# Eight expert tiles started beside the last routing tail, two softmax inverses on VectorE, and store landings awaited one tile later

## The reference

```python
# 1. attention over pixels with 128 inner channels, then 1x1 convolutions, a residual and relu
attn = softmax(einsum('bcn,bcm->bnm', v, q), axis=2); av = einsum('bcn,bnm->bcm', k, attn)
x = relu(bn2(conv(bn1(conv(av)))) + x)
t = to_tokens(x)                                   # 4 x 1024 tokens of 256 values
# 2. eight heads of 32
t = t + attention(ln(t)) @ w_out + b_out
# 3. mixture of 8 experts, the two best experts for each token
logits = ln(t) @ Wr; top_vals, top_idx = top_k(logits, 2); top_w = softmax(top_vals)
for e in range(8):
    y = gelu(flat @ W1[e] + b1[e]) @ W2[e] + b2[e]  # 256 -> 1024 -> 256
    out = out + gates[:, e:e+1] * y
```

## Time and profile before

| what | value |
|---|---|
| median of 3 runs | 1309.75 us (1306.08 to 1310.2) |
| the profiled execution | 1310.52 us |
| its span | 1308.7 us |
| busy: TensorE | 1151.3 us, 88% |
| busy: VectorE | 792.5 us, 61% |
| busy: ScalarE | 630.8 us, 48% |
| busy: GpSimd | 577.6 us, 44% |

### The profile page before, as it was taken

How to read it: one execution, slowest core, us unless ns; L and a number is a source line. 1 busy time by engine, 2 the same in 40 slices (tenths; PEclk the granted TensorE clock), 3 DMA queues, 4 the chain that set the end, 5 groups by cost and what they waited for, 6 DMA issues and landing times. The chain is left out here.

```text
span 1308.7 us, 29280 instructions
## 1 busy us (share of the span) xinstructions
PE 1151.3 (88%) x10343; PEld 759.2 (58%) x10343; DVE 792.5 (61%) x1425; ACT 630.8 (48%) x1129; POOL 577.6 (44%) x455
## 2 busy tenths in 40 slices
PE   3999799996589999999999998159999999999993
PEld 2555454644334444445445444049999999998772
DVE  2546545565578878778877871735565556555540
ACT  0636356464257756775776675223333333333332
POOL 1314224241358865276257526434444444444330
PEclk9989899896679999999999999569999999999996
DMA  4126652443412323232142413712333323332227
GB/s 125 50 65 208 272 168 88 139 144 110 129 41 55 79 77 73 73 97 90 43 110 78 106 43 100 269 34 41 49 50 49 51 49 50 49 50 43 41 32 263
DMA packets 99246, 120.47 MB, mean 92 GB/s; under 512 B 29400, under 2 KB 76440, under 8 KB 98488
## 3 DMA queue, kind: packets, MB, share of 16 engines
q1 hardware_dynamic: 78152, 70.29, 18.3%
q0 software_dynamic: 20544, 42.22, 14.5%
q10 hardware_dynamic: 432, 6.29, 1.2%
HBM read 72.97 MB, written 45.60 MB: 91 GB/s over the span
## 5 line engine op out<-in xcount | busy, mean ns | idle before, releaser
L823 ACT ACTIVATE WB<-PP 128x512 f32<-128x512 f32 x512 | 268.5, 606 | 167.5 <-PE PP L1132 167.4
L1449 DVE TENSOR_REDUCE mxp<-PP 128x2 f32<-128x1024 f32 x256 | 301.3, 1218 | 66.4 <-PE PP L1065 65.1
L868 ACT ACTIVATE WORK<-PP,b1c 128x256 f32<-128x256 f32 (+1 forms) x320 | 143.5, 449 | 258.4 <-PE PP L896 254.8
L633 POOL TENSOR_TENSOR WB<-WB 128x1024 f32<-128x1024 f32 x80 | 188.6, 2358 | 79.5 <-PE PP L1121 71.3
L896 PE MATMUL PP<-WORK,WB 128*128 128x256 f16 (+1 forms) x1920 | 207.9, 264 | 3.2 <-DVE WORK L1750 3.1
L1244 PE MATMUL PP<-WB,WORK 128*128 x1704 | 193.8, 273 | 0.0
L896 PEld LDWEIGHTS PP<-WORK,WB 128*128 x1920 | 176.6, 99 | 29.6 <-issue 4.2
L1244 PEld LDWEIGHTS PP<-WB,WORK 128*128 128x128 f16 x1704 | 164.4, 98 | 20.9 <-issue 0.4
L1132 PE MATMUL PP<-WORK 97*128 97x256 f16 x1024 | 160.6, 281 | 8.5 <-ACT WB L823 5.4
L601 POOL TENSOR_TENSOR WB<-WORK,WB 128x1024 f16<-128x1024 f32 x32 | 68.1, 2129 | 218.4 <-ACT WORK L734 218.4
L697 POOL DMA_INDIRECT res_d<-WORK,lb x71 | 115.7, 1630 | 102.8 <-DVE WORK L1777 87.5
(11 more groups left out here) (255 smaller groups left out, 1169.4 us busy)
## 6 DMA issues: line engine op xcount, KB each, us to landing
WORK<-in_L_ffn_W_dram POOLq DMA_DIRECT2D x32, 512.0 KB, 4.3
res_d<-WORK SPq DMA_DIRECT2D x8, 1024.0 KB, 4.5
late_d<-WB POOLq DMA_DIRECT2D x1, 6144.0 KB, 18.7
WB<-late_d ACTq DMA_DIRECT2D x3, 2048.0 KB, 17.8
WORK<-in_x_dram SPq DMA_DIRECT2D x8, 512.0 KB, 3.8
v_d<-WORK SPq DMA_DIRECT2D x4, 1024.0 KB, 4.8
WORK<-q_hi_d SPq DMA_DIRECT2D x16, 256.0 KB, 3.9
WORK<-v_d SPq DMA_DIRECT2D x8, 512.0 KB, 5.6
```

The source lines that it names most:

```text
L633: pool.tensor_tensor(PS[n % 2], PR[n % 3][:, 0], PR[n % 3][:, 1], ALU.add).then_inc(s("pair_kept"), 1)
L823: act.activation(PR[n % 3][:, c // 2, c % 2 * 2:c % 2 * 2 + 2], SCORES[m % 3] .rearrange("p (h n) -> p h n", h=2), ACT.Exp).then_inc(s("e_ ...
L868: act.activation(hid[u][:, k, 0:width], hidden_bank(k)[:, 0:width], ACT.Gelu, bias=b1c[:, bass.ds(e, 1), k], scale=1.0 / WSCALE)\
L1449: dve.tensor_reduce(mxp[:, n // 4 % 2, i, h:h + 2, k], PP[2 + h // 2][:, :].rearrange("p (h n) -> p h n", h=2), X_AXIS, ALU.max).then_inc( ...
```

## The change

Six things change. The diff has some 900 lines; the core follows the list, sorted by engine.

- **Eight early tiles.** In steps 21 to 27 of the last batch, VectorE computes a first table from the lists' counts of batches 0 to 2 (`early_table`): the first 8 whole lists of 256, in the experts' order. These are tiles 0 to 7. The table of the other 32 is computed from the counts of all batches less those 8, in four parts behind the outputs of tiles 1 to 4 (`count_lists`, `place_pairs`, `singles_near`, `singles_far`). The number of tiles stays 31 + 9.
- **The last tail is woven into tiles 0 to 4** on every engine. TensorE ranks in the middle of first(0), ScalarE normalises two token blocks behind each of the gelus of tiles 0 to 3, and VectorE splits their rows (`tail_low`). GpSimd writes its 16 pieces of the lists as 4, 3, 3, 3, 3 in its turns 0 to 4.
- **One buffer `hid`** instead of two takes the gelus; a pair of chunks is written when VectorE has split the same pair of the tile before. The loops of VectorE and ScalarE over the tiles are written out.
- **The last two units of the attention** are inverted and multiplied by VectorE (`finish_unit`), the last straight from PSUM.
- **The weights of experts 5 to 7** come back in three loads as before, one semaphore each; the buffers that lie in their place in phase B are exchanged, so that expert 7 is the last to come. TensorE waits for all three before first(2).
- **`output_landed`** waits for a tile's store behind the next tile's gather and pieces, instead of straight behind the store.

```diff
+WHOLE = B * 8 - 2
+EARLY = 8
+LAST_PIECES = (0, 4, 7, 10, 13, 16)
+COUNT_AT, EARLY_AT = 21, (21, 22, 23, 24, 25, 26, 27)
...
 # SyncE
-            spread_inverses(B * UNITS - 2)
-
-            store_rows(B - 2, B - 1)
-            sp.wait_ge(s("pv_made"), FREE + STEPS * B)
...
-            store_res1(B - 1, B)
-            store_rows(B - 1, B)
-            sp.wait_ge(s("st_res1"), FREE + 16 * B)
-            sp.wait_ge(s("st_rows"), 16 * B)
-            sp.wait_ge(s("ld_nm"), 32 * UNITS * B)
-            sp.wait_ge(s("st_list"), 16 * 2 * NT * B)
-            sp.wait_ge(s("table_kept"), 1)
...
+            sp.wait_ge(s("early_kept"), 1)
+            sp.wait_ge(s("st_list"), 16 * 2 * NT * (B - 1))
+            for t in range(LISTS):
+                load_list(t)
+            store_res1(B - 1, B)
+            sp.wait_ge(s("ld_p0"), 16)
+            sp.sem_inc(s("late_on"), 1)
...
+            for t in range(LISTS, EARLY):
+                load_list(t)
+            store_rows(B - 1, B)
+            sp.wait_ge(s("st_res1"), FREE + 16 * B)
+            sp.wait_ge(s("st_rows"), 16 * B)
...
+            sp.wait_ge(s("st_list"), 16 * 2 * NT * B)
+            sp.wait_ge(s("table_kept"), 1)
+            for t in range(EARLY, PAIRS):
+                load_list(t)
...
 # GpSimd
-            normalise(B * UNITS - 2)
-            normalise(B * UNITS - 1)
-            scatter(B, range(2 * NT))
...
-                pool.wait_ge(s(f"st_y{u}"), rows_loaded(t))
+
+            def output_landed(t):
+                pool.wait_ge(s(f"st_y{t % 2}"), rows_loaded(t))
                 pool.sem_inc(s("y_out"), 1)
...
             for t in range(TILES):
                 if t + 3 < TILES:
                     gather(t + 3)
+                if t + 1 < len(LAST_PIECES):
+                    at, end = LAST_PIECES[t:t + 2]
...
+                    scatter(B, range(at, end))
+                if t:
+                    output_landed(t - 1)
                 store_output(t)
...
 # ScalarE
+                for k in range(HC):
+                    if t and k % 2 == 0:
+                        act.wait_ge(s("hs_kept"), FREE + 4 * (t - 1) + k // 2 + 1)
...
+                gelus(t)
+                if t == 0:
+                    act.wait_ge(s("st_res1"), FREE + 16 * B)
+                if t < NT // 2:
+                    norm_pair(t)
...
 # TensorE
+                if t < 2:
+                    pe.wait_ge(s("late_on"), pe.value_load(tile_need[0:1, t:t + 1], min_val=FREE, max_val=FREE + LATE))
+                elif t == 2:
+                    pe.wait_ge(s("late_on"), FREE + LATE)
                 for k in range(HC):
+                    if t == 0 and k == 4:
+                        tail_ranks(B - 1, FINAL_SLOTS, B)
...
 # VectorE
+            for part in range(4):
+                tail_pick(part, B)
+                if part == 1:
+                    keep_turned(0, 0)
...
+            tail_gates(B - 1, B)
+
+
             split_hidden(0, 0)
             keep_turned(1, 1)
...
+                    split_hidden(t + 1, (t + 1) % 2, t + 1 < PAIRS)
+                if t < NT // 2:
+                    tail_low(t)
+                if t + 2 < TILES:
+                    keep_turned(t + 2, t % 2, t + 2 < PAIRS)
...
+                keep_output(t, t % 2, e, t, t < PAIRS)
+                if t == 1:
+                    count_lists()
+                if t == 2:
+                    place_pairs()
+                if t == 3:
+                    singles_near()
+                if t == 4:
+                    singles_far()
```

More of the change, by code:

```diff
@@ L69 @@
           "hs_kept st_out0 st_out1 st_out2 st_out3 f_kept qhi_kept qlo_kept vt_kept_a vt_kept_v idx_kept "
[L70 removed]
+          "nrm_kept sum_kept y_kept f_out st_q0 st_q1 y_made y_out late_on")
 def max_groups(t, first, last):
@@ L499, in attend @@
                           .then_inc(s("ld_res0"), 16)
+                    if k == 7 and last:
+                        store_rows(b - 1, b)
             store_max(0, 0)
@@ L621, in _ @@
                 pool.memset(two4[:, k:k + 1], float(2 * k + 2))
+            for k in range(E):
+                pool.memset(seq8[:, k:k + 1], float(k))
             pool.memset(step8, 0.0)
@@ L860, in _, with norm_pair @@
-            act.wait_ge(s("table_kept"), 1)
-            def gelus(t, u, at, wide=True):
-                width = TT if wide else P
-                e = act.value_load(tile_e[0:1, at], min_val=0, max_val=E - 1)
+            def norm_pair(part):
+                for t in (2 * part, 2 * part + 1):
+                    op = act.activation(t1[:, t], t1[:, t], ACT.Identity,
+                                        bias=small[:, 4, t:t + 1], scale=small[:, 3, t:t + 1])
+                op.then_inc(s("ln1_kept"), 1)
+                tail_high(part, B, t1[:, 2 * part:2 * part + 2])
@@ L1165, in attend @@
                             tail_ranks(b, before, b)
+                        if last and t == COUNT_AT:
+                            tail_count(b, before, b)
             for name, n in (("vt_kept_v", 1), ("vt_kept_a", 1), ("qlo_kept", 4)):
@@ L1590, in attend @@
                         tail_gates(b - 1, b)
+                    if last and t in EARLY_AT:
+                        early_table(EARLY_AT.index(t), before)
             for n in range(4):
@@ L1620, in _ @@
-            tail_gates(B - 1, B)
-            for part in range(NT // 2):
-                here = slice(2 * part, 2 * part + 2)
-                dve.wait_ge(s("hi_kept"), 4 * (B - 1) + part + 1)
-                dve.tensor_tensor(rows[:, here, 1, :], ln_last[:, here], rows[:, here, 0, :], ALU.subtract)\
-                   .then_inc(s("rows_kept"), 1)
-            dve.wait_ge(s("zero_kept"), 1)
-            dve.wait_ge(s("cnt_made"), 1)
-            dve.tensor_copy(cnt, PP[0][:, 0:E])
-            dve.tensor_copy(seqc, seq.bitcast(I32))
@@ new lines, in tail_low @@
+            def tail_low(part):
+                here = slice(2 * part, 2 * part + 2)
+                dve.wait_ge(s("hi_kept"), 4 * (B - 1) + part + 1)
+                dve.tensor_tensor(rows[:, here, 1, :], t1[:, here], rows[:, here, 0, :], ALU.subtract)\
+                   .then_inc(s("rows_kept"), 1)
+            for c in range(NT):
+                tail_project(c, before, B)
+                tile_statistics(c)
+            dve.drain()
+            deviations("stat1_kept")
+            for part in range(4):
+                tail_pick(part, B)
+                if part == 1:
+                    keep_turned(0, 0)
@@ L1785, in _ @@
+            tail_rstd(B)
+            tail_pick(4, B)
+            for part in range(3):
+                tail_places(part, before, B)
+            tail_gates(B - 1, B)
             split_hidden(0, 0)
             keep_turned(1, 1)
-            with dve.Fori(0, (PAIRS - 1) // LISTS) as i:
-                for j in range(LISTS):
-                    u, t = j % 2, i * LISTS + j
-                    e = expert(bass.ds(t, 1))
+            for t in range(TILES):
+                e = expert(slice(t, t + 1))
+                if t + 1 < TILES:
```

474 lines of the change are left out of this document (267 added, 207 removed).

## The result

| kernel | median | runs | ratio to before, 95% interval |
|---|---|---|---|
| before | 1309.28 us | 4 (1306.08 to 1310.2) | |
| changed | 1278.49 us | 4 (1275.03 to 1282.47) | 0.9768 (0.975 to 0.9785) |

The forecast was 1284, range 1275 to 1297. The profiled execution of the changed kernel took 1282.47 us, the longest of the four; its span is 1280.4.

A forecast was written before the change was run, and what follows sets the result against it. Phase C is bound by TensorE, after a hole where tile 0 waited 31.91 us for gathered tokens. Span 1308.7 - 33.3 + 7.6 - 1.4 = 1281.6, with 1.8 outside 1283.4, taken as 1284 us; range 1275 to 1297.

The forecast's parts named there:

- two small stalls: Waits of TensorE from VectorE's two middle table parts, within tiles 2 to 6: 0.4 us each.
- Until first(2): Start of phase C through tiles 0 and 1: first(2) at 853.5 instead of 886.76, a gain of 33.3 us.
- Tiles 2 to 6 give some of it back: GpSimd's ring and VectorE's table parts stretch these tiles: stalls of 3.4, 0.4, 0.4 and 3.4, together 7.6 us lost.
- S + 13.9: In tiles 2 to 6, VectorE's output is done 13.9 us after first(t+1) starts at S; GpSimd's ring takes 12.35.
- What stays hidden: Early table, tail_low, norm_pair, last pieces and late weights cost nothing extra; tile 8's list is ready about 11 us early.
- The landing awaited later: Later wait for each store: nothing in steady tiles (ring 8.9 under 10.93), gain 1.4 us at the change to single tiles.
- Until the first copy: nothing: Before tile 0's copy, new inverses cost nothing and tile 0's tokens are there: xT kept at 826.0.
- Rival C: Early gathers and residual store run late beside 6 MB of weights: 12 us more, 1296; chance 0.11.
- The rule on the shared port: VectorE copies lock GpSimd out of descriptor writes: an estimated 70 us lost over four rings; the forecast kept 1.03 per piece.
- Rivals D: Gathers and pieces slow to 1.69 us beside VectorE: 14 us more, 1298; chance 0.05, of which 0.01 slower.
- E: Ring around y_out outgrows a tile of TensorE, so every tile pays: at ring 12.0, 40 us, 1324; chance 0.04.
- F: No effect: the wait only moves to tile 8, whose list needs the last batch: 1309; chance 0.05.

The follow-up runs named there:

- pieces first: Changed kernel with 12 of the last batch's 16 list pieces in GpSimd's turn 0 and 4 in turn 1, none in turns 2 to 4: 1281.75 us.
- tile 1's copy first: Changed kernel with VectorE copying tile 1's turned tokens ahead of tile 0's four pairs instead of behind them: 1273.46 us.
- weights first: Changed kernel with TensorE waiting for all three late weight loads ahead of first(0): 1285.09 us.
- tile 0 behind the tail: Changed kernel with tile 0 not woven into the tail: ranks ahead of first(0), tile 0's copy behind the gates: 1283.47 us.
- both inverses as before: Changed kernel with inverses and products of the attention's last two units done the way of the kernel before: 1293.46 us.
- The three runs: Changed kernel with old inverses for units 30 and 31, for unit 31 only, and for both with SyncE's old order: 1293.46, 1299.63 and 1306.41 us.
- copy earlier: Changed kernel with table parts ahead of outputs, tile 1's copy ahead of tile 0's pairs, plus tile 0's copy ahead of the choice of experts: 1269.73 us.
- the landing at once: Changed kernel with each store's landing awaited straight behind the store, as in the kernel before: 1285.25 us.
- unit 31 alone: Changed kernel with only unit 31 put back to ScalarE's copy, VectorE's inverse and GpSimd's product; unit 30 stays on VectorE: 1299.63 us.
- both units with the order as before: Changed kernel with both units' old inverses, and batch 2's rows stored behind the transfers of unit 30's inverse: 1306.41 us.

## Why the prediction was right, and where its terms were off

| step | forecast | trace |
|---|---|---|
| first(0), first(1), first(2) | 826.6, 840.7, 853.5 | 827.4, 840.87, 853.79 |
| gain to first(2) | 33.3 | 33.0 |
| first stall, first(4) | 3.4 | 1.6 |
| two small stalls | 0.8 | 0 |
| last stall, first(7), and its clock | 3.4 | 2.2 + 1.7 |
| single tiles | 1.4 | 1.15 |
| span | 1281.6 | 1280.4 |
| median of the kernel | 1284 | 1278.49 |

**Until first(2)** the sum held to 0.3 us, though phase B ended 0.8 later: against its last matmuls the gain is 33.75. The half clock cost what it had cost at each restart, 1.8 us in half of first(0) and 2.0 in first(1).

**"Tiles 2 to 6 give some of it back"** is the step that was mis-sized: 7.6 against 5.5, and of the 5.5 only 3.8 are stalls; 1.7 is tile 7's clock, for which the sum had no term. The place and the cause (a table part in front of the pairs) were right, and moving the table ahead of the outputs removed all of it.

The closeness of 5.5 is in part luck. Five other traces with the same two stalls (pieces first, tile 1's copy first, weights first, tile 0 behind the tail, both inverses as before) show no fall of the clock at tile 7. They take 69.2 to 69.5 us from first(2) to first(8), 3.6 to 4.0 more than the 65.56 without stalls: half of the 7.6. The profiled execution is also the longest of its four, so its span lies nearer the forecast than the median does, which is 5.5 below. Nor do the recorded terms give 7.6: put into the sum as it stands, with S + 13.9, the four parts make stalls of 3.2, 1.9, 1.6 and 3.6, over 10 us. The 0.4 of the middle two comes out only with the output done near S + 12.4, so without the ring that the other two have.

Two terms were too large. The output was put at S + 13.9, from a ring of 12.35 around GpSimd that I took as binding. It came at S + 12.6 (866.4 less 853.79), and the run with the pieces first shows that the ring is no part of it. The four pairs take 4.6 us back to back, not 5.05: the 1.31 of the earlier trace rows includes waits for the gelus, which were all done here when the pairs began. These two make most of the 1.8 by which the first stall was too large, and the small ones vanish with them.

**"What stays hidden"** held: gather(8) went out at 906.89 for a turn at 919.16. **The landing awaited later** was called nothing in wide tiles. That was true of steady tiles only; in the turns with pieces it is worth 4.4 us, as its undoing shows.

**"Until the first copy: nothing"** came out right: the copy ends at 826.57 (825.89 and 0.68), 13.44 us behind the last matmuls, where the forecast of 826.0 is 13.65 behind them. But it did so for a reason that I had not named. I put the new inverses at nothing, because VectorE's additions start at the same place, and I used that the gather goes out early without pricing what happens if it doesn't. Rival C had that kind of mechanism, small transfers late beside the weights, at a chance of 0.11. The three runs show its price: one product more on GpSimd in front of the first gather 3.3 us, the old transfers of unit 30 another 10, whether the rows' store stood ahead of them or behind. In the changed kernel gather 0 is issued at 813.23 and the first weights at 813.89.

**The rule on the shared port** (the Trainium skill, SBUF — State Buffer, section "SBUF: two separate sides") does not show in any of the runs: the 16 pieces took 974 ns each beside VectorE's copies and casts, less than the 1031 ns beside the table. The longest indirect DMA in all traces is a store of 2.10 us (pieces first, at 857.12), where most stores take 1.6. The groups by line of GpSimd from 836 to 902 in the changed kernel (count, busy us, mean ns):

```profile
L682 POOL DMA_INDIRECT list_d<-meta,idx x16 | 15.6, 974 | 6.7 <-issue 4.6 <-DMA list_d<-meta,idx 2.1
```

The late small transfers do agree with another page. The Trainium skill (DMA: Bandwidth & Descriptors, section "Queues, rings and completion order") says that each DMA engine takes turns between the queues that have work for it, a packet at a time. The trace agrees in kind: loads of 3 KB that land in 2.0 us with no weights under way needed 16.5 beside 2 MB loads on another queue. No run shows the turns themselves.

Rivals D, E and F have no support: pieces and gathers kept their length, steady tiles are 10.93 us apart, and no wait moved to tile 8.

## What to carry to other kernels

When work is started early beside a big load, list every small transfer that it hangs on (tokens, lists, partial results) and have each issued ahead of the load: here a gather issued 4.0 us later, and so behind the load, cost 3.3 us, and the small transfers of one unit another 10. Where side work must run on an engine that also feeds the bound one, put it in front of the instruction that waits for the bound engine, not behind it; that alone gave 3.8 us, and 5.5 where a stall had also cost the clock. And release the bound engine's next input before the work that only a later stage needs: 5.2 us for two exchanged lines.

## What was not expected of the hardware

The granted clock of TensorE doesn't follow the last gap alone. It fell behind gaps of 2.02 us (changed kernel, tile 7) and 2.11 us (inside first(0), copy earlier), but not behind the gaps of 1.34 to 1.88 in front of tiles 4 and 7 of the other runs, not in the 2.8 us behind 2.08 (same run, ahead of first(0)), and not behind 2.17 in the run with the landing at once, where first(7) took 5.43 us behind two gaps of 2.17 and 1.59. The clearest pair is first(4) in the last two runs, unit 31 alone and both units with the order as before:

```profile
891.25 6.74 PE L933 MATMUL PP<-WORK,WB 128*128 128x256 f16 x48 [2.98 <-DVE WORK L1719]
...
898.67 5.43 PE L932 MATMUL PP<-WORK,WB 128*128 128x256 f16 x48 [2.97 <-DVE WORK L1712]
```

Behind the same gap the granted clock is 0.50 in the first (891.2 to 894) and 1.00 in the second (898.7 to 901). A tile that starts after a fall took 6.7 to 8.0 us instead of 5.40. What decides at gaps of 2 to 3 us stays open. So does the cause of the pauses on the last chip.
